# An attention and FFN block on one core: batch 0 ahead of the other batches, row maxima half a batch ahead, identity products while TensorE has nothing else

## Chip, core and metric

The kernel runs on one NeuronCore of a Trainium2 chip. The metric is the device time of one execution in microseconds (us). Engines are named as in the profile: PE (TensorE), DVE (VectorE), ACT (ScalarE), POOL (GpSimd), SP (SyncE, which issues all DMAs here).

## What is computed

Eight batches of 512 rows with 256 features. Each row is normalised (mean 0, variance 1), and the block returns x + attention(xn) + ffn(xn). The attention has 16 heads of 16 features, rotary positions and a causal mask; the ffn is one 256x256 product of values that are quantised to fp8 with one scale for the whole tensor, so the largest absolute value of all eight batches must be known before any output row can be finished.

```python
xn = _layernorm(x)                                  # (8, 512, 256)
Q, K, V = xn @ W_q.T, xn @ W_k.T, xn @ W_v.T        # 16 heads of 16
scores = einsum(rope(Q), rope(K)) * 16 ** -0.5      # causal
heads = softmax(scores) @ Vh
x + heads @ W_o.T + fake_quant_fp8(xn) @ fake_quant_fp8(W).T + bias
```

## The kernel before

**Precision by parts.** Q and K of a head are rotated in fp32 and then written as three bf16 parts each (high, middle, low). The parts go to DRAM (`qk_parts`) and come back as "stacks": `q_st` and `k_st` hold, for each head, 96 rows of parts so that one bf16 product of 96 rows gives scores of nearly fp32 precision. There are two copies of both stacks, for even and odd batches.

**Maxima first.** The softmax needs each row's maximum. PE computes the scores once in one orientation (`scores_for_max`, L860, into three PSUM banks `s_ps`) and DVE reduces them to `rowmax` (`row_max`, L587). PE turns `rowmax` (`turn_max`, L907), DVE splits it into two bf16 rows (`split_max`, L623 and L625), and SP writes them to DRAM and reads them back as two more rows of `q_st` (`shift_rows`, L366 and L370), for half of the heads at a time. Then PE computes the scores in the other orientation with 98 rows (L842, into two banks `st_ps`), so that the maximum is already subtracted; ACT takes the exponent (L722), POOL zeroes what the causal mask hides (L427), and PE multiplies by V (`pv`, L922). ACT copies the heads out (L737), PE turns them (L878), DVE divides by the sums (L597, L601), PE turns them again (L886), ACT copies (L743), PE does the output product together with the ffn (L894, L899), DVE adds it to the residual `x_res` (L610), and SP stores 512 KB.

**Slots and stages.** A batch is 20 slots (`SLOTS`); each has two halves of exponents (two banks of L842 and L722) and two banks of maxima. Four stages overlap: in iteration b, stage 1 projects batch b + 2 (L798, rotation L510, L511, L252, L253 and the three parts), stage 2 takes the maxima of batch b + 1, stage 3 the exponents of batch b, and stage 4 finishes batch b - 1. `MISC` says in which slot each smaller PE item comes ("qk" projections, "v", "o" turned heads, "at", "fin", "mt" turned maxima); these share the two banks `m_ps`. Iterations run from -1 (maxima of batch 0 alone) to 8 (batch 7 is finished, nothing else). Each engine executes its own queue in order, and the engines are tied by semaphores alone.

**Start.** `each_batch` loads and normalises all eight batches one after another: DVE statistics (L485 to L496), POOL the inverse root (L398, L400), ACT normalises (L657), PE turns the rows (L782), ACT copies them to `xnT` (L666), and DVE takes the largest absolute value (`largest`, L500). After batch 3's statistics DVE rotates the first projections. PE takes the first maxima only when all eight batches are in `xnT`. In iteration -1, `weight_step` forms the fp8 scales and quantises the ffn weights. POOL sets the rows of ones that `k_st` needs (L473).

**Quantised input.** For each batch ACT scales `xnT` (`qv`, L754), DVE forms `qe` (L640, L644), and POOL adds and subtracts (L453, L457) to give `xq`. POOL adds the bias to the residual (L448).

## Time and profile before

| | us |
|---|---|
| median of 3 runs | 469.36 (468.85 to 469.9) |
| profiled execution, device time | 468.62 |
| its span, first to last instruction | 466.9 |
| PE busy | 405.5 (87%) |
| DVE busy | 350.1 (75%) |
| ACT busy | 277.3 (59%) |
| POOL busy | 274.4 (59%) |

How to read it: the page gives busy time, then the span in 40 slices with busy tenths, the granted clock of TensorE and the DMA load; then the chain that ended last and the costliest groups. The view of windows gives the same busy times for stretches that one chooses. The timeline lists instructions in order of time; what stands in brackets is the idle time of the engine before a row and who ended it. A matmul of fp32 operands shows as two instructions.

### The profile page before, as it was taken

Reading aid. Unit: us, or ns where it says so; the run is one execution under the profiler, and the core shown is the slowest. Engines: PE = TensorE matmul, PEld = TensorE weight load, DVE = VectorE, ACT = ScalarE, POOL = GpSimd, SP = SyncE. Lnnn points to the kernel's source line nnn. Section 1 sums busy time; section 2 is a strip of 40 time slices with the busy share of each in tenths; the row PEclk is TensorE's granted clock in tenths of the full one; section 3 lists DMA queues with packets and bytes.
Section 4 is the critical chain, followed back from the end, with each engine's and each line's share of the span. In section 5 each row is a group of like instructions: output and inputs, shape, how many; then the busy total and the mean of one; then the engine's idle time right before and its main releaser. Section 6 shows DMA issues by size and latency. Waiting matters only on the chain.

```text
span 466.9 us, 9145 instructions
## 1 busy us (share of the span) xinstructions
PE 405.5 (87%) x2819; PEld 222.8 (48%) x2819; DVE 350.1 (75%) x1340; ACT 277.3 (59%) x500; POOL 274.4 (59%) x278
## 2 busy tenths in 40 slices
PE   1790676999889999999999999999999999998975
PEld 1440521364345556654565556555655545643443
DVE  3779899969769977997799778977897878842041
ACT  2742932147765677567666765677567656675850
POOL 2304376636746984698459844985498337226552
PEclk9996555599999999999999999999999999999999
DMA  7826747300483238422851375037504760020021
GB/s 234 257 87 197 159 136 193 81 5 18 143 214 84 69 101 204 131 69 78 216 144 46 93 213 152 32 110 206 158 18 124 194 170 2 4 93 3 1 91 46
DMA packets 37617, 53.43 MB, mean 114 GB/s; under 512 B 5152, under 2 KB 31136, under 8 KB 37536
## 3 DMA queue, kind: packets, MB, share of 16 engines
q1 hardware_dynamic: 37568, 52.84, 40.6%
q8 instruction: 23, 0.38, 0.3%
q14 instruction: 26, 0.21, 0.2%
HBM read 35.78 MB, written 17.04 MB: 113 GB/s over the span
## 4 chain that ended last, share of the span: by engine, by line
PE 44%; POOL 22%; ACT 11%; issue 10%; DVE 8%; DMA 3%; POOLq 1%; SPq 1%; ACTq 0%; DVEq 0%
PE st_ps L842 10%; PE o_ps L922 9%; PE s_ps L860 7%; ACT prob L722 6%; PE m_ps L894 5%; PE m_ps L869 4%; POOL prob L427 4%; POOL rot L259 4%; PE m_ps L798 4%; POOL rot L253 3%; DVE scratch L587 3%; POOL xq L457 3%; POOL parts L263 3%; POOL rot L252 2%; POOL qv L453 2%
## 5 line engine op out<-in xcount | busy, mean ns | idle before, releaser
L587 DVE CUSTOM_DVE_ANT_0 scratch<-s_ps,causal 128x512 bf16<-128x512 f32 (+3 forms) x512 | 220.9, 485 | 55.0 <-PE s_ps L860 52.9
L722 ACT ACTIVATE prob<-st_ps 128x512 f32<-128x512 f32 x320 | 174.8, 600 | 97.9 <-PE st_ps L842 97.4
L427 POOL TENSOR_SCALAR_AFFINE_SELECT prob<-prob 128x512 f32<-128x512 f32 (+1 forms) x160 | 86.4, 544 | 130.9 <-ACT prob L722 129.4
L860 PE MATMUL s_ps<-k_st,q_st 96*128 96x512 bf16 (+3 forms) x512 | 130.8, 320 | 7.0 <-DVE rowmax L587 3.2
L842 PE MATMUL st_ps<-q_st,k_st 98*128 98x128 bf16 (+3 forms) x512 | 121.9, 303 | 4.2 <-ACT prob L722 2.8
L922 PE MATMUL o_ps<-prob,v_sb 128*17 128x512 f32 (+3 forms) x1024 | 87.4, 437 | 10.0 <-ACT heads L737 5.1
L842 PEld LDWEIGHTS st_ps<-q_st,k_st 98*128 98x128 bf16 x512 | 42.0, 97 | 76.3 <-ACT prob L722 42.3
L860 PEld LDWEIGHTS s_ps<-k_st,q_st 96*128 96x128 bf16 x512 | 48.9, 99 | 43.7 <-DVE rowmax L587 20.6
L922 PEld LDWEIGHTS o_ps<-prob,v_sb 128*17 128x17 f32 x1024 | 20.5, 96 | 48.3 <-issue 36.0
L587 DVE DVE_READ_ACCUMULATOR2_ANT rowmax<- 128x1 f32 x512 | 41.7, 81 | 0.1
L894 PE MATMUL m_ps<-wo_sb,attnT 128*128 128x256 f32 x128 | 33.2, 381 | 1.8 <-DVE x_res L610 1.4
L263 POOL TENSOR_TENSOR parts<-rot,parts 128x1024 bf16<-128x1024 f32 x14 | 29.9, 2133 | 5.4 <-ACT parts L675 5.4
L610 DVE SCALAR_TENSOR_TENSOR x_res<-m_ps,both,x_res 128x256 f32<-128x256 f32 x32 | 15.4, 480 | 23.3 <-PE m_ps L899 20.3
L869 PE MATMUL m_ps<-wv_sb,xnT 128*128 128x256 f32 x128 | 32.1, 396 | 0.0
L259 POOL TENSOR_TENSOR rot<-rot,parts 128x1024 f32<-128x1024 f32 x14 | 29.9, 2136 | 1.5 <-ACT parts L671 1.5
L252 POOL TENSOR_TENSOR rot<-prod 128x512 f32<-128x512 f32 x14 | 17.8, 1271 | 19.3 <-DVE prod L511 19.2
L675 ACT CAST parts<-rot 128x1024 bf16<-128x1024 f32 x15 | 15.7, 1047 | 19.7 <-POOL rot L259 15.8
L782 PE MATMUL st_ps<-ident,prob 128*128 128x128 f32 x32 | 6.9, 388 | 23.3 <-ACT prob L657 23.3
L869 PEld LDWEIGHTS m_ps<-wv_sb,xnT 128*128 128x128 f32 x128 | 24.8, 199 | 4.2 <-DVE x_res L610 0.2
L671 ACT CAST parts<-rot 128x1024 bf16<-128x1024 f32 x15 | 15.8, 1054 | 17.5 <-DMA qk_parts<-parts 8.8
L894 PEld LDWEIGHTS m_ps<-wo_sb,attnT 128*128 128x128 f32 x128 | 22.7, 189 | 5.6 <-DVE x_res L610 1.8
L737 ACT COPY heads<-o_ps 128x512 f32<-128x512 f32 x32 | 19.0, 594 | 9.5 <-PE m_ps L878 9.0
(99 smaller groups left out, 502.6 us busy)
## 6 DMA issues: line engine op xcount, KB each, us to landing
qk_parts<-parts SPq DMA_DIRECT2D x16, 768.0 KB, 3.7
q_st<-qk_parts SPq DMA_DIRECT2D x32, 192.0 KB, 3.3
k_st<-qk_parts SPq DMA_DIRECT2D x32, 192.0 KB, 3.7
q_st<-x_dram SPq DMA_DIRECT2D x8, 512.0 KB, 5.5
q_st<-qk_parts SPq DMA_DIRECT2D x32, 128.0 KB, 3.4
k_st<-qk_parts SPq DMA_DIRECT2D x32, 128.0 KB, 3.7
x_res<-x_dram SPq DMA_DIRECT2D x8, 512.0 KB, 3.5
out_dram<-x_res SPq DMA_DIRECT2D x8, 512.0 KB, 4.8
```

The costliest lines, as they stand in the source:

```text
L252: eng.tensor_tensor(dst[:, 0, :], prod[:, 0, :], prod[:, 2, :], ALU.subtract).then_inc(rotated, 1)
L259: eng.tensor_tensor(buf, buf, parts[:, w, 0], ALU.subtract).then_inc(rem_done, 1)
L263: eng.tensor_tensor(parts[:, w, 2], rotated_in(n, w), parts[:, w, 1], ALU.subtract).then_inc(low_done, 1)
L427: eng.affine_select(out=ap, in_=ap, compare_op=ALU.is_ge, fill=0.0, base=0, pattern=pat, channel_multiplier=-1).then_inc(masked, 1)
L587: eng.tensor_tensor_reduce(scratch[:, at, col:col + w], s_ps[at][:, col:col + w], causal[:, T - w:T], 1.0, NEG, ALU.add, ALU.max, rowmax[: ...
L722: eng.activation(prob[u][:, half * T:(half + 1) * T], st_ps[ST_BANK[2 * s + half]][:, :], ACT.Exp, scale=SCALE).then_inc(exp_done, 1)
L737: eng.copy(heads[:, g, :], o_ps[:, :]).then_inc(heads_copied, 1)
L842: mm = eng.matmul(st_ps[ST_BANK[i]][:, col:col + T - kb * P], k_st[0:ROWS + SHIFT, par, h, kb * P:(kb + 1) * P], q_st[0:ROWS + SHIFT, par, ...
L860: mm = eng.matmul(bank[:, col:col + (qb + 1) * P], q_st[0:ROWS, 1 - par, h, qb * P:(qb + 1) * P], k_st[0:ROWS, 1 - par, h, 0:(qb + 1) * P] ...
L869: mm = eng.matmul(bank[:, t * D:(t + 1) * D], xnT[:, c, b * T + (2 * i + t) * P:b * T + (2 * i + t + 1) * P], wv_sb[:, c, :], start=(c == ...
L894: eng.matmul(bank[:, 0:D], attnT[:, qb % 2, c, :], wo_sb[:, c, :], start=(c == 0), stop=False)
L922: mm = eng.matmul(o_ps[32 * i:32 * i + VW, kb * P:T], v_sb[:, kb, g * HG + i, :], prob[u][:, col:col + T - kb * P], start=(kb == 0), stop= ...
```

## The change

The stages and iterations are gone; every engine walks one list of slots from -10 to 178, in which batch n's exponents are in slots 20n to 20n + 19.

- **Maxima** of a slot are those of the slot that comes 10 later (`LEAD`), where it was 20. So slots -10 to -1 hold maxima alone, and slots 150 to 159 exponents alone. The small items have offsets from 20n (`OFFSETS`); projections are clipped to slot -10.
- **Batch 0 first.** x is loaded straight into `xnT` (normalised in place), all loads issued at once. Batches 0 to 2 are normalised ahead; batches 3 to 7 are normalised, turned and copied in slots -10 to -3 (`TURN_SLOT`), between maxima. Only batch 0 is projected ahead; batch 1 goes by the ordinary projection (L798 before) in slots -10 to -5. The parts of batch 0 are made in halves.
- **Moved:** the eight `largest` reductions go to slots 1, 3, ..., 15, the weight steps to slots 16 to 21; POOL's and ACT's steps on Q and K, the quantisation and the residual have slots of their own. The ones of `k_st` are set in two halves.
- **Maxima rows:** turned four times a batch rather than twice, and `shift_rows` copies each row by two DMAs inside SBUF (16 source partitions to one) rather than out to DRAM and back. The scores wait for it once per group of four heads (slots 0, 5, 10, 15).
- **SP:** the residual's load stands ahead of the stack writes and reads of its slot. The last batch uses other buffers for its residual and its `xq`, prepares both in slots 146 to 157, and is stored in four pieces.
- **Identity products:** `keep_busy` gives PE 26 products of the identity before batch 0's rows are turned and 8 behind them.

```diff
+LEAD = 10
...
+OFFSETS = {("v", 0): 0, ("mt", 1): 1, ("v", 1): 3, ("o", 0): 23, ("o", 1): 24, ("o", 2): 25, ("o", 3): 26, ("mt", 2): 7,
+           ("at", 0): 28, ("qk", 0): -32, ("at", 1): 29, ("qk", 1): -30, ("fin", 0): 31, ("at", 2): 32, ("mt", 3): 12,
+           ("qk", 2): -27, ("fin", 1): 34, ("at", 3): 34, ("qk", 3): -25, ("fin", 2): 36, ("mt", 0): -4, ("fin", 3): 38}
+SPREAD = [(17, "spread", 0, 0), (18, "spread", 0, 1)]
+TURN_SLOT = {3: -10, 4: -9, 5: -7, 6: -5, 7: -3}
...
+FIRST_SLOT, END_SLOT = -LEAD, SLOTS * NB + 19
...
+QUANT_STEPS = ("qv", "qe", "qc", "qw", "xq")
...
+    first, last, loop = (23, 24, 25, 26, 28), (6, 7, 11, 12, 14), (16, 17, 21, 22, 24)
+    return [n for n in range(NB) if SLOTS * n + (first if n == 0 else last if n == NB - 1 else loop)[k] == slot]
...
+        def xq_of(n):
+            return xq if n < NB - 1 else parts[:, 0, 0]
+        def residual_of(n):
+            return x_res if n < NB - 1 else prod[:, 0:2, :].rearrange("p a (u d) -> p (a u) d", d=D)
...
+            def load_x(n):
+                eng.dma_start(x_of(n), x[n].rearrange("(n p) d -> p n d", p=P)).then_inc(x_in[n], 16)
...
+            def shift_rows(n, g):
+
+                c = NG * n + g
+                eng.wait_ge(shift_done, c + 1)
+                for t in range(SHIFT):
+                    eng.dma_start(q_st[ROWS + t:ROWS + t + 1, n % 2, g * HG:(g + 1) * HG, :],
+                                  shift[:, t, :]).then_inc(shift_in[c % 2], 16)
+
+            def load_residual(n):
+                if n < NB - 1:
+                    wait_past(eng, y_out, 16 * n)
+                else:
+                    eng.wait_ge(rotated[1], 2 * NB)
+                eng.dma_start(residual_of(n)[:, :, :], x[n].rearrange("(n p) d -> p n d", p=P)).then_inc(res_in, 16)
...
+            load_x(0)
+            for dst, src in ((wq_sb, wq), (wk_sb, wk)):
+                eng.dma_start(dst, src.rearrange("(c p) r m -> p c r m", p=P)).then_inc(w_qk_in, 16)
+            eng.dma_start(cos_sb[:, :], cos).then_inc(w_qk_in, 16)
+            eng.dma_start(sin_sb[:, :], sin).then_inc(w_qk_in, 16)
+            for n in range(1, NB):
+                load_x(n)
+            for dst, src in ((wf_sb, wf), (wv_sb[:, :, :], wv), (wo_sb[:, :, :], wo)):
+                eng.dma_start(dst, src.rearrange("(c p) n -> p c n", p=P)).then_inc(w_in, 16)
+            eng.dma_start(bias_sb[:, :], bias.partition_broadcast(P)).then_inc(w_in, 16)
+            for w in range(2):
+                write_parts(0, w)
+            for g in range(2):
+                for w in range(2):
+                    read_stack(0, w, 0, slice(HG * g, HG * (g + 1)), first_in[g])
+            for w in range(2):
+                read_stack(0, w, 1)
+
+            for slot in range(FIRST_SLOT, END_SLOT):
+                n = residual_at(slot, 20, 14)
+                if n is not None:
+                    load_residual(n)
+                for g, off in enumerate((-3, 2, 8, 13)):
+                    n = batch_at(slot, off)
+                    if n is not None:
+                        shift_rows(n, g)
+                for off, step in ((-24, lambda n: write_parts(n, 0)), (-19, lambda n: write_parts(n, 1)),
+                                  (-18, lambda n: read_stack(n, 0, 0)), (-16, lambda n: read_stack(n, 1, 0)),
+                                  (-12, lambda n: read_stack(n, 0, 1)), (-11, lambda n: read_stack(n, 1, 1))):
+                    n = batch_at(slot, off, 1)
+                    if n is not None:
+                        step(n)
+                n = batch_at(slot, 39)
+                if n is not None and n < NB - 1:
+                    store(n)
+            store(NB - 1)
+            eng.wait_ge(y_out, 16 * (NB - 1 + NQ))
 
...
+            for n in range(3):
+                invert(n)
+            eng.wait_ge(ln_rstd, 6)
+            fill_ones(0)
+            eng.wait_ge(consts, 7)
+            remainder(eng, 0, 0)
+            low(eng, 0, 0)
+            split_weights(0)
+            split_weights(1)
+            split_x(1)
+            for n in range(3, 6):
+                invert(n)
...
+                for off, step, w in ((-29, rotate, 0), (-27, remainder, 0), (-25, low, 0),
+                                     (-24, rotate, 1), (-22, remainder, 1), (-20, low, 1)):
+                    n = batch_at(slot, off, 1)
+                    if n is not None:
+                        step(eng, n, w)
...
+            for n in range(4):
+                statistics(n)
+            eng.wait_ge(w_qk_in, 16 * 4)
+            rope(0, 0, first_ps[0])
+            rope(0, 1, first_ps[1])
+            rotate(eng, 0, 0)
+            rope(0, 2, first_ps[2])
+            rope(0, 3, first_ps[3])
+            rotate(eng, 0, 1)
+            remainder(eng, 0, 1)
+            low(eng, 0, 1)
+            for n in range(4, NB):
+                statistics(n)
...
+                if slot in range(1, 2 * NB, 2):
+                    largest(slot // 2)
+                weight_step(slot)
...
+                if c > 0:
+                    eng.wait_ge(shift_in[(c - 1) % 2], 32 * ((c - 1) // 2 + 1))
...
+            normalise(0)
+            copy_turned(0)
+            normalise(1)
+            normalise(2)
+            high(0, 0)
+            copy_turned(1)
+            middle(0, 0)
+            high(0, 1)
+            middle(0, 1)
...
+            def keep_busy(count):
+
+                for _ in range(count):
+                    eng.matmul(s_ps[2][:, 0:P], ident[:, :], ident[:, :], start=True, stop=True)
...
+            def scores(n, s, between):
+
+                g, u = divmod(s, 5)
+                if u == 0:
+                    c = NG * n + g
+                    eng.wait_ge(shift_in[c % 2], 32 * (c // 2 + 1))
...
+            keep_busy(26)
+            turn_rows(0)
+            keep_busy(8)
+            for k in range(4):
+                project_whole(k)
+            turn_rows(1)
+            turn_rows(2)
+            for slot in range(FIRST_SLOT, END_SLOT):
+                if slot == 0:
+                    eng.wait_ge(xnT_copied, 2 * NB)
+                    eng.wait_ge(consts, 9)
...
```

## Rows read from the trace of the kernel before

**Rows 1.** The page, slices: TensorE's granted clock in tenths, 40 slices of 11.67 us.
```profile
PEclk9996555599999999999999999999999999999999
```
**Rows 2.** Windows: busy us (x instructions) of each engine, granted clock, DMA share.
```profile
core 0: us, PE busy (x) PEld busy (x) DVE busy (x) ACT busy (x) POOL busy (x), PEclk, DMA share, GB/s
...
31.60:48.80 17.20, 4.86 (x15) 2.52 (x13) 15.04 (x42) 7.06 (x12) 5.24 (x7) 0.67 0.65 195
48.80:58.90 10.10, 6.70 (x27) 5.09 (x28) 7.29 (x17) 9.58 (x19) 4.17 (x5) 0.50 0.63 136
58.90:90.50 31.60, 23.95 (x68) 5.73 (x67) 31.35 (x137) 6.32 (x10) 24.03 (x12) 0.50 0.58 151
90.50:133.60 43.10, 40.44 (x274) 20.39 (x272) 34.09 (x146) 28.42 (x50) 23.90 (x28) 0.94 0.23 69
...
229.40:276.60 47.20, 45.56 (x348) 26.66 (x347) 39.33 (x155) 31.25 (x57) 33.63 (x32) 1.00 0.45 124
...
371.00:412.50 41.50, 40.40 (x324) 22.24 (x322) 33.87 (x147) 26.46 (x52) 17.75 (x23) 1.00 0.25 64
412.50:448.30 35.80, 32.74 (x256) 16.21 (x254) 6.29 (x16) 26.26 (x52) 17.06 (x22) 1.00 0.10 32
448.30:466.90 18.60, 10.15 (x74) 6.68 (x72) 6.54 (x15) 3.12 (x7) 7.68 (x4) 1.00 0.25 85
```
**Rows 3.** Timeline of the first 25 us: start, duration, engine, line, operation, count.
```profile
7.96 2.07 ACT L657 ACTIVATE prob<-q_st,shift_x,rstd 128x256 f32<-128x256 f32 x4 [5.88 <-POOL shift_x L400]
...
10.18 1.94 PE L782 MATMUL st_ps<-ident,prob 128*128 128x128 f32 x8 [10.18 <-ACT prob L657]
...
14.90 1.40 DVE L485 BATCH_NORM_STATS2 stats<-q_st 128x6 f32<-128x256 f32 x4
...
15.39 1.04 ACT L666 COPY xnT<-st_ps 128x512 f32<-128x512 f32 x2
...
17.29 5.15 PE L789 MATMUL m_ps<-xnT,prob 128*128 128x512 f32 x8
...
20.84 0.69 DVE L510 TENSOR_TENSOR prod<-m_ps,cos_sb 128x512 f32<-128x512 f32 x1 [2.86 <-PE m_ps L789]
...
22.28 1.04 PE L782 MATMUL st_ps<-ident,prob 128*128 128x128 f32 x8
```
**Rows 4.** Timeline from 32 to 59 us: the parts out, the stacks in, the first maximum.
```profile
32.45 0.37 SPq L328 DMA_DIRECT2D qk_parts<-parts  x1
...
36.17 2.67 SPq L359 DMA_DIRECT2D q_st<-qk_parts  x6
...
38.88 0.42 SPq L340 DMA_DIRECT2D qk_parts<-parts  x1
...
43.49 4.01 SPq L359 DMA_DIRECT2D k_st<-qk_parts  x9
...
58.89 0.69 DVE L587 CUSTOM_DVE_ANT_0 scratch<-s_ps,causal 128x512 bf16<-128x512 f32 x1 [2.27 <-PE s_ps L860]
```
**Rows 5.** Timeline of DVE in the maxima alone: the same bank, five banks apart.
```profile
81.37 0.67 DVE L587 CUSTOM_DVE_ANT_0 scratch<-s_ps,causal 128x512 bf16<-128x512 f32 x1
...
84.66 0.67 DVE L587 CUSTOM_DVE_ANT_0 scratch<-s_ps,causal 128x512 bf16<-128x512 f32 x1
```
**Rows 6.** Groups by line: count, busy us, mean ns, idle before and releaser.
```profile
L259 POOL TENSOR_TENSOR rot<-rot,parts 128x1024 f32<-128x1024 f32 x14 | 29.9, 2136 | 1.5 <-ACT parts L671 1.5
...
L798 PE MATMUL m_ps<-x_parts,wq_parts 128*128 128x512 f32 x72 | 20.0, 413 | 0.0
...
L500 DVE TENSOR_REDUCE amax<-prob 128x1 f32<-128x1024 f32 x8 | 9.7, 1207 | 1.4 <-ACT prob L657 1.4
```
**Rows 7.** DMA issues: count, KB each, median us from issue to landing.
```profile
shift_rows<-shift SPq DMA_DIRECT2D x16, 16.0 KB, 3.1
```
**Rows 8.** Timeline of the last 9 us.
```profile
458.12 0.48 DVE L610 SCALAR_TENSOR_TENSOR x_res<-m_ps,both,x_res 128x256 f32<-128x256 f32 x1 [2.99 <-POOL x_res L448]
...
463.57 0.38 SPq L319 DMA_DIRECT2D out_dram<-x_res  x1
```

988 lines of the change are left out of this document (442 added, 546 removed).

## Prediction

> **What bounds the kernel now.** I read the slices of the page first: the clock row says that TensorE's clock is granted at half (1.2 instead of 2.4 GHz) from within slice 3 to within slice 8, about 38 to 95 us [rows 1]. Then I cut the span at the first exponent of each batch and asked for busy time by window [rows 2]. The reader should see five regimes. (a) To 58.9 us no maximum is taken: the start. (b) From 58.9 to 90.5 DVE is busy 31.35 of 31.60 us: maxima of batch 0 alone, DVE-bound. (c) Batch 0's exponents, 43.1 us, without a batch to finish. (d) Full batches, 47.2 us each (batches 1 to 5; the first two took 48.3 and 47.5), with PE busy 45.56: PE-bound. Batch 6 has no projections and takes 41.5 us, batch 7 has no maxima either and takes 35.8. (e) A tail of 18.6 us. So the sum is 58.9 + 31.6 + 43.1 + 48.3 + 47.5 + 3 x 47.2 + 41.5 + 35.8 + 18.6 = 466.9 us. The change can't take PE work out of (d); it can take out (a), (b) and parts of (e).
>
> **The start, to the first maximum.** Batch 0 is normalised by 10.0 us and turned by 12.1 [rows 3]. Before, ACT first normalised batch 1 and copied batch 0's turned rows at 15.39; now the copy follows at once and ends near 13.3, so the first projection is there by 15.1 at half clock or 14.3 at full (two instructions of 512 columns each 0.86 or 0.43 us: eight took 5.15 us across the switch [rows 3]). But DVE is the later one: its statistics of batches 0 to 3, of which the fourth began at 14.90 with two reductions `largest` in front [rows 3], end near 15.8 without them. From there DVE has four rope pairs (1.3 us each; one is 0.69 us [rows 3]), two rotations of the same size, and a remainder and a low in halves (1.2 us each plus ACT's copies): 15.8 + 6 x 1.3 + 2.6 = 26.2 us. POOL's half (2.14 us an operation, XX6, in halves behind ACT's) ends near 24.2. Before, these two were at 32.4 and, with the queue, 38.9 [rows 4]. A write of parts lands 3.7 us after its issue (32.45 to 36.17 [rows 4]) and up to 4.6 (38.88 to 43.49); the loads of all x and weights, 6.1 MB by the tensors' sizes, are in the queues until 31 us at the 195 GB/s of the window from 31.6 on [rows 2], earlier if the empty start moves more; so I take 30.5 to 32 for the keys, 1.4 us to issue three reads and 3.5 to land: first maximum at **37**, from 35 (no queueing) to 41 (all of it). DVE is ready by 36, since `statistics` of batches 4 to 7 waits for POOL's `invert`, which is behind `split_x`. Against 58.89 [rows 4]: -21.9 us.
>
> **The identity products.** They can only help batch 0's transposes (1.94 us at half clock against 1.04 [rows 3]) and projections. As DVE sets the pace up to the first maximum, I cost both groups at nothing; if DVE weren't the cover, they would be worth 0.9 + 4 x 0.86 / 2, about 2.6 us, in the best case. What happens to the clock afterwards is not theirs: PE now has nothing to do from about 20 to 36 us. In the trace before, PE was busy for 4.86 of the 17.2 us from 31.6 on; the granted clock was 0.67 on average in that window and 0.50 throughout the next two [rows 2], though PE had work in them. So I expect half clock again at the first maximum. The Trainium skill (TensorE: Matmul & The Clock Gate, Why this matters for your kernels) says that a pause of PE between bursts puts the clock back to half; by that rule the early products are spent before they are needed, and the trace agrees with its 0.67 and 0.50.
>
> **Slots -10 to -1.** DVE's pace in maxima alone is five banks in 84.66 - 81.37 = 3.29 us, 1.32 a slot [rows 5]; plus four rope pairs 5.2 and one `split_max` 0.6: 19 us if nothing else waits, the lower bound (20). PE at half clock has 20 banks x 0.43 = 8.6, five batches of transposes x 1.94 = 9.7, 24 product instructions of 512 columns at about 0.43 = 10.4: 29 us, the upper bound (31 with starts). At full clock it is half of that. In (c) the mean of 0.94 means half clock for (1 - 0.94) x 2 x 43.1 = 5 us and then the full one, with PE dense throughout [rows 2]; slot -10 is dense (0.9 + 1.9 + 2.6 + 2.6 us), so I take the full clock from slot -9. Sum: slot -10 ends for DVE 7.5 us in, nine slots of 1.32 = 11.8, two rope pairs 2.6, waits for the chain ACT copy 1.04, ACT normalise 2.07 [rows 3], PE turn in slots -7 and -5 about 2, and 1.6 from the last maximum to the first exponent: **25.5**. The first exponent's shift rows (slot -3) have three slots, 4 us, and need 0.9 to issue and 3.1 to land [rows 7]: just hidden. Against 31.6: -6.1 us.
>
> **Batch 0.** Here DVE takes over what (a) and (b) lost: 20 slots x 1.32 = 26.4, eight `largest` x 1.21 = 9.7 [rows 6], four rope pairs 5.2, weight steps 31.35 - 26.4 - 0.6 = 4.4 [rows 2], four `split_max` 2.3, together 48.0, and 1 us of waits: **49**, against 43.1: +5.9. It is from 45 (reductions fit in gaps: DVE had 9 us idle in this window) to 53.
>
> **Batches 1 to 6.** PE work per batch is the same but for two more small transposes. POOL has the same 33.6 us in better spread slots, except in batch 1, where `wf_q`, `split_x`, `qv`, `xq` and the residual's bias come in slots 21 to 29. I take batch 1 at 48.8, batches 2 to 5 at 47.7 (+0.5 for new waits, below), batch 6 at 41.8. Against 48.3 + 47.5 + 3 x 47.2 + 41.5 = 278.9, this gives 281.4: +2.5, from -6 to +9.
>
> **Batch 7 and the tail.** Ten slots still have maxima, so it lies between 41.5 and 35.8 [rows 2]: **38.5**, +2.7 (36 to 40). In the tail POOL's work is gone, but it delayed only the first of the four finishing steps, by 0.6 us (458.12 behind 457.5 [rows 8]); the last 512 KB were issued at 463.57 and the span ended 3.3 us later [rows 8]; a quarter of it should land 0.8 us sooner. 18.6 becomes **17.2**, -1.4.
>
> **New waits.** Scores wait for `shift_in` 32 times where it was 16 times, with 3 to 4 slots between turn and use where it was about ten. Behind that wait on PE are the maxima, so DVE, and the exponents. A group's path is DVE's split about 2 us into the slot, 0.9 to issue two DMAs, and at most 3.1 to land, what the copy to DRAM took [rows 7]; a copy inside SBUF isn't in this trace, its bounds are 0 and 3.1, and I take 3.1, the nearest row, of the same size: 6 us, against three slots of 47.2 / 20 = 2.36, 7.1 us on average and less where they hold few small items, as slots 7 and 12 do. That is why I charge 0.5 us a batch. On SP the residual's load waits for the store's landing, about 3 us, with the key parts and group 1's shift rows behind it; those land near +9 to +11 us, the scores need them at +12: hidden, with little to spare. In DVE's queue `split_max` waits for the preceding copy; it is long there.
>
> **Sum.** -21.9 - 6.1 + 5.9 + 2.5 + 2.7 - 1.4 = -18.3. The profiled execution of before took 468.62, which gives 450.3; the median is 0.74 above it, so 451 us. The ends of the terms, taken together as independent, give 441 to 463.
>
> **Rivals.**
> (1) The loop gets faster: spreading POOL's long operations returns PE's 1.6 us of idle time in each of six batches (45.56 of 47.20). For: POOL rows stand in the chain of (d). Against: the same number of them must pass. 451 - 9.6 = 441. Chance 0.20.
> (2) The clock stays at half through slots -10 to -1, as it did in (b) with PE 24 of 31.6 us busy: 31 instead of 25.5, so 457. For: that window. Against: there was no dense stretch in it. Chance 0.13.
> (3) The stack's first reads queue behind x and the weights: the first maximum at 45, so 459. For: 6.1 MB in one go. Against: in [rows 4] reads followed a write in 3.7 us under load. Chance 0.10.
> (4) Slower than before: shift rows come late. Each of 32 waits costs PE t us; the gain of 18.3 is gone at t = 0.57. At 0.8 us the time is 451 + 32 x 0.8 = 476 (less the 3 charged, 473). For: 6 us of path against 7 of cover, which a light slot uses up; SP blocked by the store. Against: DVE still has two slots of maxima in hand behind the split. Chance 0.07. The Trainium skill (DMA: Bandwidth & Descriptors, Rules for kernel authors) speaks on that side: transfers under 64 KB are mostly overhead and should be merged; here 16 KB pieces become smaller ones. By it the landing stays at the 3.1 us that the trace shows and the number of waits counts; no run here shows it for copies inside SBUF.
> (5) The change doesn't do what it says: the identity products don't move the first maximum. That is in my forecast (priced at zero), and would give the same 451.
>
> **How the numbers follow.** The forecast of 451 has 0.50. Range 437 to 463: it takes in rivals 1, 2 and 3 and leaves out 4 and the far ends. A measurement of this kernel can tell about 0.2%, 1 us. Slower by more than that: most of rival 4, 0.05; within it 0.02; faster 0.93.
>
> **What would show it.** After: first maximum at 37 us and first exponent near 62; DVE over 95% busy in batch 0's window of 49 us and PE not; windows of full batches at 47 to 48 us with PE the busiest; half clock at the first maximum and full clock within 6 us of it; POOL without work in the tail. It would be wrong if PE shows idle time ended by DMAs into `q_st` at each fifth slot, if the first maximum comes after 41, or if batch 0 takes under 45.

## The result, and the profile after

The changed kernel takes 465.55 us (median of six runs, 462.89 to 466.08) where the kernel before took 468.75 in the same session: a ratio of 0.992, interval 0.9895 to 0.9944. The prediction was 451 us with a range of 437 to 463. The sign is right, the gain is 3.2 us where 18 was forecast, and the time lies outside the range. (In the prediction's paragraph on the start, "XX6" is a slip for [rows 6].) All times and ratios here are of executions in the chip's fast state; one slow execution each of e9 (461.38 us) and e14 (672.25 us) is left out.

The profiled run of the changed kernel took 465.83 us, span 463.4. I cut it as the span of before was cut: start, maxima alone, batch 0, batch 1, a full batch, batches 6 and 7, tail. Columns as in [rows 2].

```profile
core 0: us, PE busy (x) PEld busy (x) DVE busy (x) ACT busy (x) POOL busy (x), PEclk, DMA share, GB/s
0.00:40.20 40.20, 22.40 (x118) 17.71 (x119) 28.21 (x96) 19.39 (x34) 22.98 (x31) 0.81 0.76 232
40.20:67.30 27.10, 20.26 (x102) 13.95 (x100) 20.20 (x82) 17.09 (x31) 17.30 (x13) 0.90 0.39 89
67.30:118.50 51.20, 44.66 (x278) 22.16 (x279) 46.49 (x164) 30.62 (x55) 26.29 (x29) 0.87 0.44 104
118.50:169.00 50.50, 47.22 (x350) 26.66 (x349) 41.94 (x160) 32.43 (x58) 36.02 (x34) 1.00 0.47 106
...
217.90:266.80 48.90, 46.84 (x349) 26.51 (x348) 40.07 (x158) 31.08 (x57) 33.64 (x32) 1.00 0.51 120
...
364.80:407.30 42.50, 39.19 (x315) 20.57 (x315) 33.01 (x141) 26.39 (x52) 19.71 (x23) 1.00 0.50 110
407.30:448.10 40.80, 36.97 (x294) 19.26 (x297) 21.88 (x89) 26.21 (x51) 24.49 (x26) 1.00 0.14 46
448.10:463.40 15.30, 10.00 (x72) 6.44 (x64) 4.66 (x12) 2.08 (x6) 0.64 (x1) 1.00 0.14 46
```

Set beside the terms of the prediction, in us:

| part | before | predicted | after | error |
|---|---|---|---|---|
| to the first maximum | 58.9 | 37 | 40.2 | +3.2 |
| maxima alone, to the first exponent | 31.6 | 25.5 | 27.1 | +1.6 |
| batch 0 | 43.1 | 49 | 51.2 | +2.2 |
| batch 1 | 48.3 | 48.8 | 50.5 | +1.7 |
| batches 2 to 5, sum | 189.1 | 190.8 | 195.8 | +5.0 |
| batch 6 | 41.5 | 41.8 | 42.5 | +0.7 |
| batch 7 | 35.8 | 38.5 | 40.8 | +2.3 |
| tail | 18.6 | 17.2 | 15.3 | -1.9 |
| span | 466.9 | 448.6 | 463.4 | +14.8 |

The first two parts gained 23.2 us, and the batches gave 23.0 of it back; the 3.3 us of the tail are what is left. The full batches are the surprise: 48.9 us each, against 47.2 before [rows 2]. Of these 1.7 us, 0.4 show as idle time of PE (1.64 to 2.06 us) and 1.3 as busy time (45.56 to 46.84), of which 0.6 are the two more turns of maxima (two products of 0.5 us in all became four of 1.1). Inside a full batch, the timeline shows a pause of PE that the kernel before didn't have:

```profile
223.25 1.89 PE L873 MATMUL m_ps<-wv_sb,xnT 128*128 128x256 f32 x8
...
226.99 1.09 ACT L712 ACTIVATE prob<-st_ps 128x512 f32<-128x512 f32 x2 [3.11 <-PE st_ps L844]
227.96 0.59 ACT L719 COPY v_sb<-m_ps 128x512 f32<-128x512 f32 x1
228.60 0.66 PE L880 MATMUL m_ps<-ident,heads 128*128 128x128 f32 x4 [1.05 <-ACT v_sb L719]
```

PE makes the second value product (L873) in slot 3 of a batch and is done at 225.1. ACT copies it out only in slot 4, behind that slot's exponents, at 227.96. The second block of turned heads (L880, also in slot 4) takes the same one of the two shared banks, so PE stands for 1.05 us. Before the change the same product stood in slot 3 too, but its bank was taken in slot 5, with a projection between. The waits hang together: PE waits for ACT, and ACT had just waited 3.11 us for PE's scores, which stand behind slot 3's product and its first block of turned heads.

### The profile page after: what moved, and what is told of

Read it like the earlier page. It is cut to its first block, busy times and chain, and to the rows that moved or that the text cites. A ratio compares the mean times of both kernels' runs of the same rounds, so it can differ in the third digit from the quotient of the medians.

```text
span 463.4 us, 9406 instructions
## 1 busy us (share of the span) xinstructions
PE 408.1 (88%) x2911; PEld 232.8 (50%) x2911; DVE 356.8 (77%) x1372; ACT 278.6 (60%) x505; POOL 282.0 (61%) x284
## 4 chain that ended last, share of the span: by engine, by line
PE 60%; DVE 16%; ACT 8%; issue 7%; DMA 4%; POOL 3%; SPq 1%; DVEq 0%; ACTq 0%; POOLq 0%
PE o_ps L931 14%; PE st_ps L844 12%; PE s_ps L864 9%; PE m_ps L829 7%; DVE scratch L600 7%; PE m_ps L873 6%; PE m_ps L896 6%; ACT prob L712 4%; PE m_ps L880 2%; DMA xnT<-x_dram 2%; PE m_ps L901 1%; DMA q_st<-shift 1%; DVE amax L538 1%; DVE rowmax L600 1%; PE m_ps L887 1%
## 5 line engine op out<-in xcount | busy, mean ns | idle before, releaser
L458 POOL TENSOR_SCALAR_AFFINE_SELECT prob<-prob 128x512 f32<-128x512 f32 (+1 forms) x160 | 90.2, 566 | 140.8 <-ACT prob L712 140.6
L864 PE MATMUL s_ps<-k_st,q_st 96*128 96x512 bf16 (+3 forms) x512 | 123.8, 304 | 23.8 <-DMA k_st<-qk_parts 14.3
L600 DVE DVE_READ_ACCUMULATOR2_ANT rowmax<- 128x1 f32 x512 | 40.8, 80 | 0.0
L313 POOL TENSOR_TENSOR parts<-rot,parts 128x1024 bf16<-128x1024 f32 (+1 forms) x16 | 32.6, 2041 | 2.4 <-ACT parts L698 2.4
L308 POOL TENSOR_TENSOR rot<-rot,parts 128x1024 f32<-128x1024 f32 (+1 forms) x16 | 32.1, 2010 | 3.0 <-ACT parts L693 3.0
L873 PE MATMUL m_ps<-wv_sb,xnT 128*128 128x256 f32 x128 | 32.0, 395 | 0.0
L548 DVE TENSOR_TENSOR prod<-m_ps,cos_sb 128x512 f32<-128x512 f32 x30 | 22.2, 798 | 9.3 <-PE m_ps L829 8.7
L880 PE MATMUL m_ps<-ident,heads 128*128 128x128 f32 x128 | 19.6, 276 | 8.7 <-ACT v_sb L719 7.4
L873 PEld LDWEIGHTS m_ps<-wv_sb,xnT 128*128 128x128 f32 x128 | 25.2, 200 | 3.1
L829 PE MATMUL m_ps<-x_parts,wq_parts 128*128 128x512 f32 x84 | 23.9, 422 | 1.8 <-DVE shift L635 1.8
L829 PE MATMUL m_ps<-x_parts,wk_parts 128*128 128x512 f32 x84 | 24.6, 430 | 0.0
L680 ACT ACTIVATE xnT<-xnT,shift_x,rstd 128x256 f32<-128x256 f32 x32 | 16.6, 593 | 10.9 <-POOL shift_x L429 10.8
L621 DVE SCALAR_TENSOR_TENSOR x_res<-m_ps,both,x_res 128x256 f32<-128x256 f32 x28 | 13.5, 481 | 11.7 <-PE m_ps L901 11.7
```

What stands on the lines that cost most here:

```text
L308: eng.tensor_tensor(buf, buf, parts[:, w, 0, a:z, :], ALU.subtract).then_inc(rem_done[w], z - a)
L313: eng.tensor_tensor(parts[:, w, 2, a:z, :], rotated_in(n, w)[:, a:z, :], parts[:, w, 1, a:z, :], ALU.subtract).then_inc(low_done[w], z - a)
L458: eng.affine_select(out=ap, in_=ap, compare_op=ALU.is_ge, fill=0.0, base=0, pattern=pat, channel_multiplier=-1).then_inc(masked, 1)
L600: eng.tensor_tensor_reduce(scratch[:, at % 3, col:col + w], s_ps[at % 3][:, col:col + w], causal[:, T - w:T], 1.0, NEG, ALU.add, ALU.max, ...
L829: mm = eng.matmul(bank[:, :], w_parts[k // 2][:, wp, c, k % 2, :], x_parts[:, xp, c, :], start=(i == 0), stop=(i == len(terms) - 1))
L864: mm = eng.matmul(bank[:, col:col + (qb + 1) * P], q_st[0:ROWS, n % 2, h, qb * P:(qb + 1) * P], k_st[0:ROWS, n % 2, h, 0:(qb + 1) * P], st ...
```

## Experiments

Times are medians. Each ratio is to the kernel before, timed in the same session: 468.71 us beside e1 to e4, 468.68 beside e5, e7, e8 and e9, 469.38 beside e6, e10, e11 and e12, and 469.32 beside e13 and e14. Differences in us between kernels of different sessions are taken as they are. The windows come from one profiled execution of each kernel, and its start differs from the next one's by up to 1.6 us for a reason outside the edits: DVE's statistics of batch 1 wait for that batch's rows and began at 10.58 us in the changed kernel, but at 9.49 in e2 and 10.90 in e6, which have the same code up to there; their first maxima came at 39.0 and 40.6.

**e1: the rows of ones by DMA.** POOL fills two rows of `k_st` with ones by two operations of 3.5 us, one in the start and one in slot -4; here four DMAs bring them from a small tile.

```diff
-            fill_ones(0)
+            for par in range(2):
+                for t in range(SHIFT):
+                    eng.dma_start(k_st[ROWS + t:ROWS + t + 1, par, :, :], ones_q[:, :])
```

> The changed kernel, but the rows of ones in k_st come by four DMAs from a small tile instead of POOL's two memsets of 3.5 us. Theory A: each memset stands on the path once. The first holds DVE's small steps (one of 0.17 us took 3.11 while the memset ran), so the first maximum comes 3 us sooner, at 37.2 instead of 40.2. The second delays POOL's rotation of batch 1's keys and, behind it, ACT's copies, which stand in ACT's queue ahead of the first exponent; so the first exponent comes another 3 to 4 us sooner, about 60.5 instead of 67.3. Time of the changed kernel less 6 to 7 us: ratio to before 0.977 to 0.980. Rival B: the start waits for DMA landings and batch 0 for DVE, so the 3.5 us are lost again to other waits; ratio 0.988 to 0.992, as for the changed kernel.

Measured: 462.92 us, ratio 0.9859, interval 0.9801 to 0.9918, which overlaps that of the changed kernel and lies between the two theories. The first maximum stays (40.0), so the first half of theory A failed: the fill in the start holds DVE's rotations by 0.6 us, not 3 (last section), and batch 1's rows came 0.3 us later here. The window of maxima alone takes 25.7 us instead of 27.1 and batch 0 49.2. In the changed kernel PE has the first exponent's scores at 63.7, but:

```profile
56.72 3.51 POOL L432 MEMSET k_st<- 2x4096 f32 x1
60.31 1.27 POOL L300 TENSOR_TENSOR rot<-prod 128x512 f32<-128x512 f32 x1
...
64.13 2.13 POOL L308 TENSOR_TENSOR rot<-rot,parts 128x1024 f32<-128x1024 f32 x1 [1.32 <-ACT parts L693]
...
66.34 1.04 ACT L698 CAST parts<-rot 128x1024 bf16<-128x1024 f32 x1 [2.38 <-POOL rot L308]
67.29 1.08 ACT L712 ACTIVATE prob<-st_ps 128x512 f32<-128x512 f32 x2
```

The fill stands in POOL's queue in front of batch 1's key rotation, that holds ACT's cast, and the cast stands in ACT's queue in front of the first exponent. In e1 the order is the same and the first exponent still follows this cast directly (65.7), so the fill was only a part of that delay.

**e2: the second value product one slot earlier.** Nothing else.

```diff
-OFFSETS = {("v", 0): 0, ("mt", 1): 1, ("v", 1): 3,
+OFFSETS = {("v", 0): 0, ("mt", 1): 1, ("v", 1): 2,
```

> The changed kernel, with the second V product of a batch one slot earlier (slot 2 instead of 3). In the changed kernel ACT copies that product a slot later, and the turned heads two items behind it in the same shared bank wait for it: PE stands still for 1.2 us once in each full batch. Theory A: PE sets the pace there, so each of batches 1 to 7 loses 1.2 us less: full batches 47.7 instead of 48.9 us, the time 8 us less, ratio 0.975. Rival B: full batches are slower for another reason (two more small transposes, more waits), and the freed 1.2 us go to the next wait in line, that for an exponent or a mask; full batches stay within 0.4 us of 48.9, ratio 0.986 to 0.992.

Measured: 451.89 us, ratio 0.9628, interval 0.9574 to 0.9683. This one digit gives 13.7 us, more than theory A's 8. (The profiled execution, 449.21 us, was the fastest of the four.) The same batch as above:

```profile
211.10:258.10 47.00, 46.30 (x349) 26.64 (x348) 39.79 (x158) 30.99 (x57) 33.65 (x32) 1.00 0.53 124
```
```profile
214.73 1.93 PE L873 MATMUL m_ps<-wv_sb,xnT 128*128 128x256 f32 x8
...
217.95 0.60 ACT L719 COPY v_sb<-m_ps 128x512 f32<-128x512 f32 x1
...
219.79 0.60 PE L880 MATMUL m_ps<-ident,heads 128*128 128x128 f32 x4
```

The turned heads follow the copy by 1.2 us and wait for nothing; PE's idle time falls to 0.70 us a batch and the batch to 47.0. It is the same pair of banks, only with one slot more between.

**e3: both.**

> Both edits together. Theory A: they are in different stretches and add up: 14 us below the changed kernel, ratio 0.962. Rival B: the ratio stays over 0.98.

Measured: 449.77 us, ratio 0.9597, interval 0.9544 to 0.9651. The expectation holds; the step from e2 is inside the intervals.

**e9: the same collision taken away on ACT's side.** PE's order stays; ACT copies the second product in its own slot.

```diff
-                for n, i in [(n, i) for _, n, i in shared_at(slot - 1, "v")]:
+                for n, i in [(n, i) for d in (1, 0) for _, n, i in shared_at(slot - d, "v") if i == 1 - d]:
```

> The changed kernel as it is (465.6 us), but ACT copies the second value product in the slot in which PE makes it, behind that slot's exponents, instead of one slot later; PE's order and the banks stay. Theory A (what the earlier product of the run before gave, 13.7 us, came from the bank that ACT's copy frees for the turned heads): the waits of 1.1 us of PE for that copy go, full batches fall from 48.9 to 47 to 47.5 us, and the time is 452 to 456. Theory B (the gain came from where the product stands among PE's work): full batches stay at 48.9 and the time within 1 us of 465.6. The copy could make the next slot's exponents late; then part of A's gain is missing.

Measured: 456.63 us, ratio 0.9735, interval 0.9696 to 0.9775; full batches 47.8. PE's wait for the copy is gone, and so are 8.9 us, with the product where it was: 1.1 of the 1.9 us a batch are shown to be the bank. The other 0.8 are not settled. The trace shows ACT standing in front of its next exponents until PE is done:

```profile
221.69 0.59 ACT L719 COPY v_sb<-m_ps 128x512 f32<-128x512 f32 x1 [1.30 <-PE m_ps L873]
```

But the product's place may cost as well. In batch 0 no turned heads follow the product (the bank's next tenant comes in slot 8), and there the move still shortened the batch from 49.2 (e1) to 48.3 us (e3), both at a mean clock of 0.98.

**e4: no products of the identity.** `keep_busy(26)` and `keep_busy(8)` are left out of the changed kernel.

> The changed kernel without its 34 identity products. Theory A (as predicted): DVE sets the pace up to batch 0's rotations, so half clock in the first transposes and projections costs nothing: first maximum within 0.5 us of 40.2, time within 1 us of the changed kernel. Rival C: they are on the path, each of the first transposes and the four projections at half clock delays the ropes; first maximum 2 to 3 us later, ratio 0.997.

Measured: 464.71 us, ratio 0.9909, interval 0.9874 to 0.9945: the same as the changed kernel. The first maximum came at 41.5 instead of 40.2, past theory A's 0.5 us; 0.8 of it is the rows of batch 1, which came at 11.34, so some 0.5 us are left for the products. The time doesn't show them.

**e5: products also in the gap.** On top of e3, 58 more behind the third batch's transposes, where PE has nothing to do until the keys land.

```diff
             turn_rows(2)
+            keep_busy(58)
             for slot in range(FIRST_SLOT, END_SLOT):
```

> The kernel with both edits (value product at offset 2, rows of ones by DMA; 449.8 us) plus 58 further products of the identity behind the third batch's transposes, which keep PE busy from about 23 to 33 us, where the trace shows it idle and the granted clock at half from 25 to 42 us. Theory A (the clock at the first maxima matters): the first maxima run at the full clock, each bank 0.22 us instead of 0.43 on PE; the first exponent comes 1 to 2 us sooner and the time is 448 to 448.8. Theory B (DVE and the parts' way through DRAM set the pace until the first exponent): the half-clock stretch goes, the first maximum stays within 0.3 us and the time is within 0.5 us of 449.8. In both the products stand behind nothing that waits; if they stand in front of the transposes of a later batch they could cost up to 1 us.

Measured: 447.3 us, ratio 0.9545, interval 0.9531 to 0.9559 (e3: 0.9544 to 0.9651, so they overlap). The maxima alone take 23.5 us instead of 25.1, at the full clock; the first maximum stays (38.9, in e3 38.7). The slices of the changed kernel's clock, and the window and slices of e5:

```profile
PEclk9956897997999999999999999999999999999999
```
```profile
38.90:62.40 23.50, 17.90 (x102) 11.88 (x100) 20.16 (x81) 17.00 (x31) 13.72 (x11) 1.00 0.43 107
```
```profile
PEclk9999999998979999999999999999999999999999
```

**e6: the residual's load where it would stand behind the stack.** In the changed kernel, `residual_at(slot, 20, 14)` becomes `residual_at(slot, 25, 14)`.

> The changed kernel (465.6 us) with one of its parts undone: SP issues the residual's load five slots later, behind the key parts and the stack's second half, not in front of them. Theory A (it is hidden wherever it stands: POOL adds the bias some slots later and the finishing steps come 11 slots later): within 0.5 us of 465.6. Theory B (where it stood it delayed the shift rows of the second group, whose landing took 3.5 to 5 us instead of 2.2 to 2.8): 1 to 4 us faster. Theory C (the finishing steps now wait for the bias): 1 us or more slower, with a wait for x_res in each batch.

Measured: 465.21 us, ratio 0.991, interval 0.9878 to 0.9943, every full batch 48.9 to 49.0: this part of the change is worth nothing either way.

**e7: shift rows written twice.** On top of e3; the first pair of copies goes to two unused rows of `q_st`. DVE's split also waits for the further copies of the groups before it.

```diff
                 for t in range(SHIFT):
+                    r = ROWS + SHIFT + t
+                    eng.dma_start(q_st[r:r + 1, n % 2, g * HG:(g + 1) * HG, :], shift[:, t, :])
+                for t in range(SHIFT):
```

> The kernel with both edits (449.8 us), in which SP writes each group's two shift rows first to two unused rows of the same tile and then to their place: four small copies where there were two, so each group's path grows by some 0.9 us of issue and perhaps some landing time. Theory A (rival 4 of the prediction, the scores live on the edge of the shift rows' arrival): each of 32 waits costs about 0.9 us more, 20 to 29 us in all. Theory B (the rows arrive 1.2 to 3.7 us before their use in full batches, with nothing in hand only for two groups of batch 0, two of batch 6 and one of batch 7): the time grows by 5 x 0.9 = 4.5 us at most and by 1 to 3 us likely.

Measured: 461.5 us, 11.7 more than e3 (ratios 0.9834 and 0.9597). The scores' waits for shift rows in e3, and then in e7 (engine and operation, what it waited for: us in total, times, longest):

```profile
PEld st_ps L841 <- DMA q_st<-shift: 4.4, 6, 1.2
...
PE st_ps L841 <- DMA q_st<-shift: 3.1, 6, 0.9
```
```profile
PEld st_ps L847 <- DMA q_st<-shift: 16.7, 16, 2.3
...
PE st_ps L847 <- DMA q_st<-shift: 13.1, 12, 2.1
```

Full batches grow by 0.2 to 1.2 us only; batches 0, 1, 6 and 7 by 3.6, 2.6, 2.3 and 1.3 (batch 0 at a mean clock of 0.93 against 0.98, so a part of its 3.6 may be the clock). Neither theory has the number: at the ends of the run, where slots are short, the rows arrive with almost nothing in hand, in the middle they have slack.

**e8: DVE's reductions cut to one element.** On top of e3. The kernel leaves out the largest value that the fp8 scale needs, so its scale isn't the reference's.

```diff
-                eng.tensor_reduce(amax[:, n:n + 1], x_of(n), AX.XY,
+                eng.tensor_reduce(amax[:, n:n + 1], x_of(n)[:, 0:1, 0:1], AX.XY,
```

> The kernel with both edits (449.8 us), whose eight reductions for the quantisation's scale look at one element of a row instead of all 1024: the scale is not that of the reference, and 9.7 us of DVE work are left out, most of it in batch 0's window. Theory A (batch 0 is bound by DVE, as the prediction's sum has it): batch 0 falls from 48.3 to about 43 us, where it stood before the change and where PE has 40.4 us of work; the time is 443 to 445.5. Theory B (batch 0 is bound by PE and the waits between the engines): batch 0 falls by under 2 us.

Measured: 446.04 us, ratio 0.9516, interval 0.9501 to 0.9531. DVE's work in batch 0 falls by 8.9 us (46.49 to 37.63), the batch by 3.5, to 44.8: between the theories. DVE bounds batch 0, but PE and the waits take over 3.5 us below. Batch 1 fell too, from 51.5 (mean clock 0.95 in e3) to 49.8, and the start of this profile was 1.9 us longer, so the total says little about batch 0.

```profile
65.70:110.50 44.80, 40.10 (x278) 20.13 (x278) 37.63 (x163) 30.44 (x54) 26.17 (x29) 0.96 0.51 119
```

**e10: two turns one slot earlier**, on top of e5: `("mt", 2)` from 7 to 6, `("mt", 3)` from 12 to 11, SP's shift rows with them.

> The kernel with both edits and the further products (447.3 us), in which the maxima of the third and fourth group are turned one slot earlier (offsets 6 and 11 instead of 7 and 12) and their shift rows follow. Theory A (the waits of PE for shift rows, 3.1 us in the trace, stand in front of those groups in batches 0, 6 and 7): 1.5 to 3 us faster, 444.3 to 445.8. Theory B (these waits are covered by others, or the earlier turns take the bank from another item): within 0.5 us. The run with the doubled copies points to A: it added 10 us to these waits and 11.7 us to the time.

Measured: 445.34 us, ratio 0.9489, interval 0.9435 to 0.9542. Batch 6 falls from 40.5 to 39.5 and full batches from 47.0 to 46.8; PE's waits for shift rows fall from 3.1 to 1.7 us in all. The interval overlaps e5's a little.

**e11: also the two steps for the scale one slot later**, 18 and 19.

> The kernel of the run before (turns one slot earlier) in which also PE's two steps for the quantisation's scale, and what follows them on DVE and ACT, stand one slot later (18 and 19 instead of 17 and 18). In the trace PE waits 1.2 and 1.1 us there for DVE, and the granted clock falls to half for 3.4 us behind it, in batch 1. Theory A: both waits and that stretch go, 2 to 4 us faster than the run before. Theory B (DVE is behind at that point anyway and PE then waits for its maxima): within 0.7 us, with the half-clock stretch still there.

Measured: 443.79 us, ratio 0.9449, interval 0.9408 to 0.9491: the fastest kernel of the study, 5.5% under before and 21.8 us under the changed one. The step from e10 (1.6 us) is inside the intervals, and the traces don't show it where the edit is: PE's two waits of 0.9 and 0.8 us are down to one of 0.3, but batches 0 and 1 together take 97.7 us against 97.8 in e10.

**e12: POOL keeps away from DVE.** In the changed kernel POOL's last step for the first queries waits until DVE is done with the first keys.

```diff
             remainder(eng, 0, 0)
+            eng.wait_ge(low_done[1], 2)
             low(eng, 0, 0)
```

> The changed kernel (465.6 us), in which POOL's last step for the first queries waits until DVE is done with the first keys, so that the two don't run at the same time. Theory A (DVE's two rotations took 1.54 and 1.64 us instead of 0.69 because POOL's operation ran beside them): both take 0.69 us, the key parts are ready 1.5 to 1.8 us sooner, near 28 us; but the queries' write is issued near 31 us instead of 26.5 and now sets the first maximum, so this comes between 38.5 and 41 us and the time is within 1.5 us of 465.6. Theory B (the durations have another cause): the rotations stay above 1.4 us.

Measured: 469.15 us, ratio 0.9993, interval 0.9963 to 1.0022. First the changed kernel, then e12:

```profile
23.73 2.72 POOL L313 TENSOR_TENSOR parts<-rot,parts 128x512 bf16<-128x512 f32 x2
...
23.90 1.54 DVE L300 TENSOR_TENSOR heads<-prod 128x512 f32<-128x512 f32 x1
25.36 1.64 DVE L301 TENSOR_TENSOR heads<-prod 128x512 f32<-128x512 f32 x1
```
```profile
23.96 0.69 DVE L300 TENSOR_TENSOR heads<-prod 128x512 f32<-128x512 f32 x1
24.57 0.69 DVE L301 TENSOR_TENSOR heads<-prod 128x512 f32<-128x512 f32 x1
...
30.88 0.96 SPq L326 DMA_DIRECT2D qk_parts<-parts  x2
```

The slow rotations are shown to be POOL's doing, and the key parts are ready 1.3 us sooner (28.5 instead of 29.8). The expectation had the queries' write near 31 us, but missed that SP writes the queries first: the keys' write stood behind the same wait for POOL, both were issued from 30.88 on, the first maximum came at 42.1 and the time grew by 3.6 us.

**e13 and e14: two statistics behind the first maxima.** On the changed kernel, and on e11.

```diff
-            for n in range(4, NB):
+            for n in range(4, 6):
                 statistics(n)
...
+                if slot in (-10, -9):
+                    statistics(slot + 16)
```

> The changed kernel (465.6 us), in which DVE takes the statistics of batches 6 and 7 behind the maxima of slots -10 and -9, not in front of all maxima. The trace has PE's first bank of scores from 37.92 us on, but DVE's first maximum at 40.24, behind 4.2 us of these two statistics, which began at 35.99 after a wait for POOL. Theory A (DVE's queue, not the keys' way through DRAM, set the first maximum): it comes at 38.3 to 38.6 us, 1.7 to 1.9 us sooner; DVE had 6.9 us idle of 27.1 up to the first exponent, so part of that stays: first exponent 0.5 to 1.8 us sooner. Theory B (the keys' landing sets it): unchanged at 40.2. In both cases the first exponent can stay where it is, at 67.3, since it waits for ACT behind POOL; then the time is within 0.5 us of 465.6.

> The fastest kernel so far (443.8 us) with the same move of two statistics. There the first bank of scores is on PE at about 37.7 us and the first maximum at 39.1, at the full clock. Theory A: first maximum at 38.1 to 38.3 us, 0.8 to 1 us sooner, and the first exponent up to 1 us sooner: 442.8 to 443.5. Theory B (the 4.2 us of statistics are only moved, and DVE's queue is what the first exponent waits for): 443.8 to 445.

Measured: e13 466.59 us, ratio 0.9933, interval 0.9908 to 0.9959; e14 449.86 us, ratio 0.9569, interval 0.9528 to 0.961, 6 us slower than e11, which neither theory had. First the changed kernel at the first maximum, then e13:

```profile
35.99 1.40 DVE L526 BATCH_NORM_STATS2 stats<-xnT 128x6 f32<-128x256 f32 x4
...
37.92 1.03 PE L864 MATMUL s_ps<-k_st,q_st 96*128 96x512 bf16 x3 [14.30 <-DMA k_st<-qk_parts]
...
38.12 1.39 DVE L526 BATCH_NORM_STATS2 stats<-xnT 128x6 f32<-128x256 f32 x4
...
40.24 0.69 DVE L600 CUSTOM_DVE_ANT_0 scratch<-s_ps,causal 128x512 bf16<-128x512 f32 x1
```
```profile
36.89 1.03 PE L866 MATMUL s_ps<-k_st,q_st 96*128 96x512 bf16 x3 [14.38 <-DMA k_st<-qk_parts]
...
37.69 0.69 DVE L600 CUSTOM_DVE_ANT_0 scratch<-s_ps,causal 128x512 bf16<-128x512 f32 x1 [2.71 <-PE s_ps L866]
```

With the statistics out of the way the first maximum follows PE's scores at 37.7 us. It comes 2.5 us sooner, but only half of that is the edit's: batch 1's rows came at 9.47 here, and e2, where they came at 9.49, has its first maximum at 39.0. The first exponent comes at 68.5 instead of 67.3: the 4.2 us of DVE work are now between them. The first maximum was a milestone, not a bound. In e14 it didn't move at all (39.3, in e11 39.1), and the first exponent came at 68.1 instead of 62.9. (The granted clock was also lower in that window; see the last section.)

## Why the prediction was wrong, point by point

**What bounds the kernel: right.** Full batches are PE-bound at 46.8 of 48.9 us, and the gain came in the first two windows and the tail only.

**New waits: this step failed, and it cost most.** It says: "That is why I charge 0.5 us a batch", and it looked only at the way of the shift rows over PE, SP and DVE. The change also re-orders some twenty small items a batch over two shared banks. I didn't walk that order and ask, for each item, when the reader of the one two places ahead of it is done. Doing so shows a copy that is one slot late. Measured: +1.7 us in a full batch against before, where +0.5 was charged. With the collision away (e2) a full batch is 47.0, under my 47.7, and batches 1 to 7 sum to 316.9 us where I had 319.9 and the changed kernel has 329.6. The 9.7 us missing in these seven batches are all there. The move of the product is worth 1.9 us a batch, of which the wait for the bank has 1.1 by e9; whether the rest is ACT's new wait or the product's place, the runs don't say. A smaller term was put at nothing: the two more turns, "two more small transposes", are 0.6 us of PE's time a batch. It didn't show against the forecast, as the waits of a full batch for POOL's mask and ACT's copy of the heads (0.8 and 0.7 us before) are gone: PE idles for 0.70 us in e2 where it was 1.64. That is the mechanism of rival 1, but with 0.7 us more of busy time it is worth 0.2 us a batch and not 1.6.

**What is luck.** e2 takes 451.89 us, and 451 was forecast. Its parts don't agree as well: by its windows the start and the maxima alone are 3.4 us over the forecast, batch 0 0.6, batches 1 to 7 3.0 and the tail 1.9 under it.

**Rival 4, shift rows late: right that they are near the edge, wrong in the place.** It priced 32 equal waits. In the changed kernel PE waits for them four times, 2.3 us in all, in batches 0 and 6. (The weight load waits once more in batch 7.) The full batches, on which the estimate rested (7.1 us of three slots), have slack; e7 and e10 show both.

**To the first maximum (+3.2): the step "DVE is ready by 36" failed.** It put all four statistics before 36; the last two start at 35.99 behind the wait for POOL and end at 40.2. The keys, which I thought decided, had PE started at 37.92 in this run and at 36.89 in e13, where my sum has them at 35.4 to 36.9. Their way has its own errors: DVE's last statistics of the first four end at 16.9 instead of 15.8 (batch 1's rows came 0.8 us later than before, at 10.58, but in e2 0.3 sooner, so that is chance of this profile), POOL's fill adds 0.6 us (last section) and its neighbouring step 1.3 (e12). In e2, with the same code, the milestone is at 39.0, +2. None of it can be added up as time: e13 moves this milestone and the kernel by nothing. Rival 3, reads of the stack that queue until 45, didn't come.

**Maxima alone (+1.6): the sum misses a queue.** I counted DVE's pace and the chain of transposes. The first exponent waited for neither, but for ACT behind POOL's fill (e1: 1.4 us less in this window). With the full clock as well it is 23.5 us (e5), 2 under my figure.

**The clock: right in what it forecast, and rival 2 fell.** Half clock at the first maximum and full within 2 us of it, at 42.0, as stated. Half clock returned in 48.9 to 52.3, 69.4 to 76.2 and 110.3 to 117.1 us; I had allowed for none of these.

**The identity products at nothing: right.** e4 differs from the changed kernel by 0.8 us, inside the intervals. The Trainium skill's rule (TensorE: Matmul & The Clock Gate, Why this matters for your kernels), that a pause of PE gives up what a warm-up won, was cited for it. e5 agrees: with the pause filled the clock stays full for the first 103 us, and the window is 1.6 us shorter. It isn't safe, though: e10 has the same 58 products, and its clock still fell to half from 39.3 to 42.7 us.

**Batch 0 (+2.2): the bound right, the clock not.** Predicted 49 by DVE's sum of 48.0; DVE was busy 46.49. In e1 and e6 the batch takes 49.2 us at a mean clock of 0.98, as predicted; in the changed kernel the mean is 0.87. There PE idles for 1.88 us, the clock falls at 69.4, and the value product takes 3.51 us where it takes 1.89 at the full clock, with the exponents behind it. e6 has the same code at this place, idles for 1.37 us and keeps the full clock; e4 idles for 1.99 and has half clock for 3.4 us, where the changed kernel has 6.8. So the cost is read from these profiles, and what sets off the fall stays open:

```profile
67.94 0.39 PE L844 MATMUL st_ps<-q_st,k_st 98*128 98x512 bf16 x1 [1.88 <-ACT prob L712]
...
72.90 3.51 PE L873 MATMUL m_ps<-wv_sb,xnT 128*128 128x256 f32 x8
...
77.76 1.09 ACT L712 ACTIVATE prob<-st_ps 128x512 f32<-128x512 f32 x2 [5.17 <-PE st_ps L844]
```

**Batch 1 (+1.7), batch 6 (+0.7), batch 7 (+2.3): the collision again.** In e2 they take 49.7, 40.2 and 38.9, against 48.8, 41.8 and 38.5 predicted. For batch 1 this isn't shown: it takes 49.9 (e4) to 51.7 us (e6) with the collision and 49.0 (e10) to 51.5 (e3, e5) without, some of them with a stretch at half clock.

**Tail (-1.9): direction right, two sizes off.** From the last DVE operation to the end of the span it is 2.1 us now against 3.4 [rows 8] (I had 0.8 less; it is 1.2). The first finishing step comes 7.7 us after the last window's start instead of 9.8; I gave POOL's absence 0.6 of that. Of the other 1.5, by the traces, 0.7 is won before PE's second turn of rows (L887, 6.2 us into the window instead of 6.9), and the rest by PE's first output product, which started at 454.56 without a wait where before it stood behind ACT's second copy of turned rows. That was read, not tried.

```profile
454.56 1.03 PE L896 MATMUL m_ps<-wo_sb,attnT 128*128 128x256 f32 x4
...
455.84 0.48 DVE L621 SCALAR_TENSOR_TENSOR prod<-m_ps,both,prod 128x256 f32<-128x256 f32 x1 [1.62 <-PE m_ps L901]
```

**The range** took in the rivals' sums but no rival in which a buffer that the change re-uses sooner costs each batch the same 2 us. Seven times 1.9, 13 us, is most of the 14.6 by which the forecast missed.

## What to carry to other kernels

When a change re-orders items that share few buffers, walk the new order by hand: for each item name the reader of the previous tenant, the slot in which that reader's engine comes to it, and what stands in front of it in its queue. Here one wait of 1.05 us, in a loop that is 96% busy on its engine, came with an order that cost 1.9 us in each of seven rounds. And don't price milestones (first maximum, last load): price what the next bound engine has to do up to the same later point, wherever the work stands.

## What the runs showed of the hardware

- DVE and POOL disturb each other only in some pairs. Two DVE rotations, both inputs in SBUF, took 1.54 and 1.64 us beside a POOL operation that reads SBUF, and 0.69 each without it (e12). DVE's rope operations, one input in PSUM, took 0.68 us beside such an operation (21.99 us, beside POOL's of 21.50). The Trainium skill (SBUF — State Buffer, Who interferes with whom) says that a DVE instruction with two SBUF inputs contends with POOL's reads and not with an instruction of POOL that only writes. The trace agrees with the first half; no DVE instruction with two SBUF inputs ran beside POOL's fills, so the second half isn't shown.
- Which of the two is held goes, in these traces, by which starts first. In e3 the rotations start at 22.49 and 23.10 us, ahead of POOL's step at 23.23; they take 0.69 each, and POOL's first operation takes 1.57 instead of 1.16. In e2 POOL starts at 23.05, between them: the first takes 0.69, the second 1.64.
- A long duration is a cost only as far as the next start is late. While POOL first filled its rows of ones (16.32 to 19.84 us), DVE shows:

```profile
16.76 3.11 DVE L533 TENSOR_SCALAR ve<-mv_b 128x4 f32<-128x4 f32 x1
...
16.91 2.97 DVE L548 TENSOR_TENSOR prod<-m_ps,cos_sb 128x512 f32<-128x512 f32 x1
17.51 2.37 DVE L549 TENSOR_TENSOR prod<-m_ps,sin_sb 128x512 f32<-128x512 f32 x1
18.11 1.77 DVE L548 TENSOR_TENSOR prod<-m_ps,cos_sb 128x512 f32<-128x512 f32 x1
18.70 1.18 DVE L549 TENSOR_TENSOR prod<-m_ps,sin_sb 128x512 f32<-128x512 f32 x1
19.98 0.69 DVE L300 TENSOR_TENSOR rot<-prod 128x512 f32<-128x512 f32 x1
```

  The rope operations (L548, L549) start 0.60 us apart, as without the fill. But all end with the fill, and the rotation, which reads their results, starts 1.28 us behind the last of them; in e1, without the fill, it is 0.72 (19.02 to 19.74). So 2.97 us shown are 0.6 us of cost. The rope operation itself isn't what the fill disturbs: beside the second fill (56.72 to 60.23 us) it takes its usual time. The row that begins the series is a small step from SBUF to SBUF, 0.17 us elsewhere; that it was held, and the ends of those behind it with it, is a reading that no run tries.

```profile
57.43 0.69 DVE L548 TENSOR_TENSOR prod<-m_ps,cos_sb 128x512 f32<-128x512 f32 x1 [0.77 <-PE m_ps L829]
```

- The granted clock makes equal code unequal. e10 and e11 have the same instructions up to slot 17, and their maxima alone took 27.1 us at a mean of 0.88 and 23.8 us at 1.00:

```profile
39.50:66.60 27.10, 21.49 (x108) 15.22 (x106) 20.12 (x80) 16.96 (x30) 13.79 (x11) 0.88 0.37 90
```
```profile
39.10:62.90 23.80, 18.09 (x105) 12.20 (x103) 20.19 (x82) 17.01 (x31) 13.74 (x12) 1.00 0.45 104
```

  A window with a half-clock stretch in one profile can't be set against one without it to 1 or 2 us; only the timed runs can, and they spread by 1 to 5 us themselves. That also bounds what e14's 6 us say: its window of maxima ran at a lower clock too (0.80 over the same stretch), which may be an effect of the moved work or chance.
